# Kept experts: when TensorE transposes the gathered tokens

## What is computed

```python
logits = where(old_to_new == -1, -inf, x @ gate_weight.T)      # 128 experts, 48 of them are kept
top_v, top_i = top_k(softmax(logits), 8)                       # 8 experts for each token
top_v = top_v / sum(top_v)
pos = place of the token in its expert's list; valid = pos < 96
xb = zeros((48, 96, 256)).at[expert, pos].set(x[tok])          # 96 tokens at most for each kept expert
g, u = split(einsum('ech,eoh->eco', xb, gate_up_proj))         # 256 -> 2 * 96
h = silu(g) * u
out = einsum('eci,ehi->ech', h, down_proj)                     # 96 -> 256
final = zeros_like(x).at[tok].add(out[expert, pos] * top_v)    # the tokens' own sums
```

## Time and profile before

| | us |
|---|---|
| median of 3 runs | 3501.74 (3493.4 to 3503.79) |
| profiled execution, its time | 3508.29 |
| its span, first to last instruction | 3506.6 |
| busy over the span: PE / DVE / ACT / POOL | 3031.0 / 1977.6 / 1560.4 / 555.3 |
| kept experts, first gather's issue to the joining DMAs | 3297.44 to 3477.32 |
| first transposes / last output product of the stage start at | 3302.48 / 3468.63 |
| joining DMAs, from their start to the end of the span | 3477.32 to 3506.6 |

### The profile page before, as it was taken

The page is one execution under the profiler, slowest core; times in us unless marked ns, Lnnn a source line. Parts: engine busy times, 40 slices in busy tenths (PEclk is TensorE's granted clock), DMA queues, the critical chain, the costliest instruction groups (busy, mean ns, idle before and its releaser), DMA issues. The chain is left out here.

```text
span 3506.6 us, 55197 instructions
## 1 busy us (share of the span) xinstructions
PE 3031.0 (86%) x18478; PEld 2325.8 (66%) x18478; DVE 1977.6 (56%) x3376; ACT 1560.4 (44%) x2702; POOL 555.3 (16%) x524
## 2 busy tenths in 40 slices
PE   5699899996984999978999999999999999963284
PEld 4434434445783777757888888888888888852153
DVE  5477667676117777774555555555555555447621
ACT  5235555554414999973333333333333333321010
POOL 3100000000013000002222222222222222100264
PEclk9779999997877999988999999999999999955555
DMA  4943443440001000000000000000000000013266
GB/s 151 224 67 51 64 62 51 66 59 17 0 13 38 0 0 0 0 9 10 9 9 9 9 9 9 9 9 9 9 9 9 9 9 7 0 50 109 61 149 123
DMA packets 155227, 132.22 MB, mean 38 GB/s; under 512 B 17487, under 2 KB 137839, under 8 KB 154555
## 3 DMA queue, kind: packets, MB, share of 16 engines
q1 hardware_dynamic: 146670, 115.81, 15.5%
q0 software_dynamic: 8448, 14.99, 2.4%
HBM read 88.87 MB, written 46.08 MB: 38 GB/s over the span
## 5 line engine op out<-in xcount | busy, mean ns | idle before, releaser
L749 DVE TENSOR_REDUCE score_pm<-score_SM 128x1 f32<-128x512 f32 (+3 forms) x673 | 429.5, 661 | 171.2 <-PE score_SM L592 102.0
L711 ACT ACTIVATE score_PR<-score_SE 128x1024 f32<-128x1024 f32 (+2 forms) x452 | 302.7, 718 | 259.3 <-PE score_SE L592 221.1
L1630 DVE SCALAR_TENSOR_TENSOR lin_go<-lin_gT,lin_O 128x512 f32<-128x512 f32 x128 | 88.0, 688 | 478.8 <-ACT lin_o L1451 478.8
L1486 PE MATMUL lin_PJ<-C_XH,lin_WH 128*128 128x512 f32 x1032 | 342.4, 413 | 13.1 <-DVE lin_WL L1590 13.1
L1415 POOL TENSOR_TENSOR lin_o2sum<-lin_o2sum,lin_o 128x512 f32<-128x512 f32 x128 | 165.7, 1294 | 1046.4 <-ACT lin_o L1451 1046.4
L1486 PE MATMUL lin_PJ<-C_XL,lin_WH 128*128 128x512 f32 x1032 | 320.8, 392 | 0.0
L1486 PE MATMUL lin_PJ<-C_XH,lin_WL 128*128 128x512 f32 x1032 | 319.8, 391 | 0.0
L590 PE MATMUL score_SM<-score_KR,score_QR 96*128 96x512 bf16 (+3 forms) x853 | 264.0, 348 | 38.4 <-DVE score_KR L772 25.5
L1647 DVE TENSOR_TENSOR lin_acc<-lin_OUT,lin_acc 128x512 f32<-128x512 f32 x256 | 177.1, 692 | 139.7 <-PE lin_OUT L1521 138.5
L1434 ACT ACTIVATE lin_qT<-lin_PJ 128x512 f32<-128x512 f32 x129 | 77.0, 597 | 379.1 <-PE lin_PJ L1486 379.1
L590 PE MATMUL score_SE<-score_QR,score_KR 99*128 99x512 bf16 (+3 forms) x772 | 213.4, 336 | 32.2 <-issue 15.0
(11 more groups left out here) (335 smaller groups left out, 6882.9 us busy)
## 6 DMA issues: line engine op xcount, KB each, us to landing
score_QR<-q_parts SPq DMA_DIRECT2D x114, 128.0 KB
score_KR<-k_parts SPq DMA_DIRECT2D x114, 128.0 KB
score_V<-v_rows SPq DMA_DIRECT2D x19, 512.0 KB
kept_GU<-L_ffn_gate_up_proj SPq DMA_DIRECT2D x48, 192.0 KB
v_rows<-qkv_vt SPq DMA_DIRECT2D x32, 256.0 KB, 2.6
C_w<-L_attn_w_qkv SPq DMA_DIRECT2D x51, 128.0 KB, 2.3
q_parts<-qkv_parts SPq DMA_DIRECT2D x16, 384.0 KB, 2.7
k_parts<-qkv_parts SPq DMA_DIRECT2D x16, 384.0 KB, 2.6
```

Of the source, the lines that this page charges most:

```text
L711: nc.scalar.activation(PR[:, (u + s) % 2, h, 0:width], SE[:, e % 2, 0:width], ACT.Exp, scale=SCALE)\
L749: nc.vector.tensor_reduce(pm[:, w, h0:h0 + nh, t, k0 // CHUNK], SM[:, p % 2, 0:nh * nk].rearrange("p (h k) -> p h k", h=nh), AX.X, ALU.max ...
L1486: ins = nc.tensor.matmul(PJ[:, bank], a[:, w, k, :], x[:, k, :, c, :], start=(n == 0), stop=(n == 3 * KD - 1))
```

## The change

Only the program of TensorE in this phase is written anew. `first` is split into `gathered` (gather wait and transposes) and `weighed` (weight wait and products). The transposes go one more expert ahead: in the loop TensorE now does the transposes of e + 2, the products of e + 1 and the output product of e. Ahead of the loop stand the transposes of experts 0 and 1 and the products of 0. GpSimd, ScalarE, VectorE and SyncE run the same programs; no buffer changes its size.

```diff
-            def first(i, u):
+            def gathered(i, u):
 
                 pe.wait_ge(g_in[u], (i + 1) * 16)
                 turn(i * S + u, u)
+
+            def weighed(i, u):
+
                 pe.wait_ge(w_in[u], (i + 1) * 32)
                 products(i * S + u, u)
 
 
-            first(0, 0)
+            gathered(0, 0)
+            gathered(0, 1)
+            weighed(0, 0)
             with pe.Fori(0, KEPT // S - 1) as i:
                 for u in range(S):
-                    first(i + (u + 1) // S, (u + 1) % S)
+                    gathered(i + (u + 2) // S, (u + 2) % S)
+                    weighed(i + (u + 1) // S, (u + 1) % S)
                     outputs(i * S + u, u)
             for u in range(S):
+                if u + 2 < S:
+                    gathered(KEPT // S - 1, u + 2)
                 if u + 1 < S:
-                    first(KEPT // S - 1, u + 1)
+                    weighed(KEPT // S - 1, u + 1)
                 outputs(KEPT - S + u, u)
```

## The result

The changed kernel takes 3555.95 us (median of 4 runs, 3552.83 to 3557.36) against 3502.53 us before (4 runs). The ratio is 1.0157, with a 95% interval of 1.0138 to 1.0176: **slower by 53 us**. The forecast was 3565.0, in a range of 3541 to 3581.

What follows compares the result with a forecast made beforehand. It took the ring of TensorE, VectorE, GpSimd and gather as the bound; 21 trips of 9.81 us, plus start and end, gave +63.3 on the 3501.7 median, 3565.0 us, range 3541 to 3581.

Steps and rivals of the forecast that it cites:

- The ring: Last computing stage: transposes T(n) to output product O, then over VectorE, GpSimd and gather to later transposes; 3.46 us per expert before.
- What goes: TensorE's 0.42 us idle before each expert's products P while ScalarE copies transposes, 20.5 in all, falls to a few.
- What comes: Ring now T(n), P(n-1), O(n-2), T(n+2): a 9.81 us trip per two experts, 4.90 per expert in place of 3.47.
- L: Path from output product O(n) through ys, scatter and gather to transposes T(n+4): taken as 8.02 us.
- the piece from T to O: TensorE's part of the new trip, from transposes through products to output product: 1.79 us.
- T to P: TensorE, from transposes to the products behind them, without the copy: taken as 0.40 us, ends 0.35 and 0.58.
- P to O: TensorE, from products to the output product behind them: 1.39 us.
- The start and the end: Stage's edges: O(0) 0.9 us late, first trip O(0) to T(4) 8.62; O(47) 6.0 after T(47).
- (a): Rival at T(n)'s gather wait: gap closes, GpSimd binds at 3.16 per expert; 12 us less, 3489; chance 0.03.
- (b): Rival: ring longer only by the step moved, gains and losses cancel; no change, 3490 to 3512 us; chance 0.04.
- (c): Rival at the gather: lands in under 2.6 us, so slower by less, 3512 to 3541; chance 0.08.
- (d): Rival on TensorE's clock: at 2.4 GHz P and T halve, 0.9 us less per trip, 3546; within the forecast's 0.81.

Runs made afterwards that it cites:

- lead-3 run of the kernel before: Kernel before, TensorE's order untouched, but GpSimd sends gathers three experts ahead instead of four: 3574.93 us, against 3506.59 on the same chip.
- lead-5: Changed kernel with eight slots instead of six and gathers five experts ahead instead of four: 3490.89 us (one run).
- eight slots and lead 6: Eight slots instead of six, gathers six experts ahead instead of four: 3485.75 us in the changed kernel, 3482.2 us in the kernel before.
- With lead 3 the new order: Changed kernel with gathers sent three experts ahead instead of four: 3741.8 us (one run).
- Without scatters: Result scatters left out, eight slots, gathers six ahead: 3479.77 us with TensorE's order of the kernel before, 3420.71 us with the changed kernel's (one run each).

## Why the prediction was right

**What bounds.** The ring, read from the chain of waits, held in every variant in which it is the longest of the bounds, and the lead-3 run of the kernel before shows it without touching TensorE. TensorE, the busiest engine, was not the bound.

**What goes.** The idle time before the products was forecast to fall to "a few"; it fell from 20.5 to 0.4.

**What comes.** One trip in two experts, with pairs: forecast 9.81, measured (3507.94 - 3311.90) / 21 = 9.34. This is the term that was mis-sized, by 21 x 0.47, or 10.0 us with the digits kept, more than the whole 9 us between forecast and median. It has two parts. L was 7.68 and not 8.02 (7.1 us in 21 trips), and all of that is the gather's own time, 3.38 for 3.74. I had named the lower load over the stage as a reason for less and given it no number. The traces show another reason: the two experts of a pair now follow one another at 2.45 (O(8) to O(9)) and not at 3.20, so the weight load behind the second output product starts mostly some 0.6 ahead of the even gather and not 0.1 to 0.2 behind it. The prediction had that load starting while the gather flies, as before, and so kept the old L. And the piece from T to O was 1.65, not 1.79 (2.9 us). T to P was right (0.37 for 0.40), but I took P to O from products that had waited for the copy, 1.39; products that don't wait need 1.28. The second T of a pair comes 2.50 behind the first, at TensorE's own pace, and not 3.2; that is outside the trip.

**The start and the end.** T(0) to T(4) took 12.8 for 14.2 forecast, since the first gather inside the loop landed faster than before (O(0) at 3305.04, T(4) at 3311.90: 6.86, not 8.62). T(46) to O(47) took 8.9 for 9.2. Together with the trips the stage is 11.7 shorter than the 229.4 forecast.

**The rivals.** (a) needed L under 5.15; with the scatters it is nowhere under 6.95. But its floor was wrong as well: GpSimd's turn is 2.97, not 3.16, so with the lead to cover it the order is worth more than I gave it. (b) is out by the result, and its price for a step by the lead-3 and lead-5 runs. (c) wanted a gather under 2.6; even without the weight loads it took 2.75, and the stage, 205.2, was 39 over before, just at the upper edge of (c). (d) I held that the clock would hardly rise with more waiting. It did rise, to 0.60 over the stage, but never in the first expert of a pair, so it didn't halve the T and P of the even ring as (d) had it. Still it had a part in the length: in the pairs of T(14), T(22), T(28) and T(36) it rose ahead of the second output product, which so came 0.2 to 0.3 earlier. The weight load behind it started 1.25 to 1.39 ahead of the next gather, and these four trips have an L of 7.07 to 7.29. The last trip, to T(46), has no weight load left beside it and 7.02; the other 16 have 7.85 on average. So 2.8 us of the 7.1 came by way of the clock, and this was luck as far as my forecast goes.

The Trainium skill ("Perfetto Trace Analysis", Identifying the Most-Contended Engine) says to optimise the engine with the highest occupancy first, but to judge TensorE by its useful work and by the busy share of its weight loads, not by that of its matmuls. My prediction left this out when it took TensorE for that engine: its weight loads are busy 97 of 180, under GpSimd's 118. By either count the rule doesn't name the ring, and the trace doesn't agree with optimising TensorE first here: the copy is hidden, and the stage has 70 us of idle time on TensorE more. In the kernel with eight slots and lead 6, where the ring is off, the same order gains 9.4 us.

## What to carry to other kernels

When a wait is moved ahead in an engine's queue, look for what stands behind it now and follows round to the same wait: count the experts (or tiles) between the send and the use, subtract how far the queue runs ahead, and divide the length of the trip by that. Running one step further ahead in the consumer costs one step of the producer's lead; give the lead back first (here two more slots), then reorder. A floor read from an engine that is paced by another is not its floor: look for a turn in which all its gaps are the smallest.

## What the runs showed of the hardware that I had not expected

TensorE's clock was at the lower level for the whole stage before, 0.50, with gaps of 0.42 us in front of each products. In the changed kernel, where TensorE is busy for less of the time, it rose in places and was 0.60 on average. Windows of the changed kernel, one pair of experts in which it rose early, from T to the end, the wait, and the next T (window, length, busy times, clock, DMA share, GB/s):

```profile
3359.50:3361.20 1.70, 1.70 (x11) 1.68 (x12) 0.00 (x0) 0.00 (x0) 0.25 (x1) 0.50 0.47 102
3361.20:3362.30 1.10, 1.10 (x6) 0.76 (x5) 0.00 (x0) 0.46 (x2) 0.00 (x0) 0.50 0.00 0
3362.30:3363.30 1.00, 1.00 (x10) 1.00 (x9) 0.70 (x3) 0.00 (x0) 0.00 (x0) 0.66 0.00 0
3363.30:3364.00 0.70, 0.63 (x5) 0.20 (x3) 0.00 (x0) 0.40 (x2) 0.24 (x1) 1.00 0.44 83
3364.00:3368.20 4.20, 0.00 (x0) 0.00 (x0) 0.70 (x3) 0.06 (x1) 3.56 (x3) 0.79 0.67 178
3368.20:3370.00 1.80, 1.74 (x11) 1.74 (x12) 0.00 (x0) 0.00 (x0) 0.93 (x1) 0.50 0.49 55
```

The clock goes to 1.00 (2.4 GHz) in this pair and is back at 0.50 (1.2 GHz) when the next one starts after the wait. Not every pair has this: of the 20 pairs from T(6) to T(45), 9 have a clock above 0.50 in the first 0.6 us of their second output product, and 11 are still at 0.50 there; all start at 0.50. With lead 3 the new order stays at 0.50 over the whole stage. Without scatters it is 0.97 with the new order and 0.50 with the old one, which has the gap of 0.42 before each products in every turn. The gap is the obvious suspect for the low clock, but the runs don't show that it is the cause: with the new order gaps of 0.40 and 0.47 in front of a T (the one at 3335.89 above) stand in a stretch at 1.00. Nor did a run hold the clock fixed, so the split of the 63 us is an estimate.

The second point is the spread of what lies ahead: the start of T(0) lies between 3288.8 and 3309.2 us in the profiles of kernels whose programs are the same up to there, more than many of the differences looked for. The stage's own length was 217.7 and 217.9 in two kernels whose totals were 3556.8 and 3567.7.
